# All ten product fields in the first step, in another order, and a quarter of the comparisons on ScalarE in three steps

## What is computed

```python
e = jnp.stack([tbl_0[ids[:, 0]], tbl_1[ids[:, 1]], ...], axis=1)   # (2048, 26, 128)
combined = jnp.concatenate([e, r_dense_x[:, None, :]], axis=1)     # (2048, 27, 128)
z = jnp.einsum('bfd,bgd->bfg', combined, combined)[:, _TRIU_I, _TRIU_J]
h = jnp.concatenate([z, r_dense_x], axis=1)                        # 351 + 128
h = jnp.maximum(h @ W_top1 + b_top1, 0.0)                          # 479 x 512
h = jnp.maximum(h @ W_top2 + b_top2, 0.0)                          # 512 x 256
y = h @ W_top3                                                     # 256 x 1
```

## Time and profile before

| | us |
|---|---|
| time, median of 3 runs (363.35 to 363.50) | 363.44 |
| profiled execution, its own time | 364.55 |
| its span, first to last instruction | 362.7 |
| PE busy | 333.9 (92%) |
| POOL busy | 255.9 (71%) |
| DVE busy | 232.7 (64%) |
| ACT busy | 130.4 (36%) |
| mean granted PE clock, share of full | 0.986 |

### The profile page before, as it was taken

One profiled execution on the slowest core, in us unless ns is written; L12 is line 12 of the kernel. 1 busy time (PEld: TensorE's weight loads), 2 busy tenths in 40 slices (PEclk: granted clock), 3 DMA queues, 4 the chain that ended last, 5 costly groups with the idle time before them and its releaser, 6 DMA issues.

```text
span 362.7 us, 9532 instructions
## 1 busy us (share of the span) xinstructions
PE 333.9 (92%) x4024; PEld 311.0 (86%) x4024; DVE 232.7 (64%) x358; ACT 130.4 (36%) x225; POOL 255.9 (71%) x271
## 2 busy tenths in 40 slices
PE   0578898999999999999999999999999999869896
PEld 0578888788999989999999989999999989858795
DVE  5998696698668928696668928695668925110010
ACT  3486364322233323332243323332343223231422
POOL 5777787777777777777777777777777777777300
PEclk9999899999999999999999999999999999978999
DMA  6998258343343414444353424343343224234220
GB/s 174 249 256 222 69 129 247 92 114 72 93 126 107 119 52 114 110 121 100 93 131 108 115 53 129 97 123 95 102 125 105 72 58 129 61 111 123 50 72 2
DMA packets 31440, 41.01 MB, mean 113 GB/s; under 512 B 16959, under 2 KB 23823, under 8 KB 31398
## 3 DMA queue, kind: packets, MB, share of 16 engines
q1 hardware_dynamic: 21827, 22.44, 22.7%
q0 software_dynamic: 8448, 17.32, 18.3%
q10 hardware_dynamic: 1123, 0.64, 0.7%
HBM read 33.01 MB, written 7.36 MB: 111 GB/s over the span
## 4 chain that ended last, share of the span: by engine, by line
PE 79%; POOL 9%; DMA 5%; issue 3%; ACT 2%; DVE 1%; ACTq 0%; SPq 0%
PE ps_o L645 35%; PE ps_g L672 16%; PE ps_l L696 10%; POOL rows L248 9%; PE ps_t L657 7%; PE ps_l L722 6%; PE ps_l L698 3%; DMA rows<-tbl,idx 3%; PE ps_l L742 1%; ACT emb L392 1%; DMA idx<-ids_g 1%; DMA turn<-gram 1%; PE ps_l L733 1%; DMA z<-turn 1%; PE ps_o L713 0%
## 5 line engine op out<-in xcount | busy, mean ns | idle before, releaser
L248 POOL DMA_INDIRECT rows<-tbl,idx x264 | 255.0, 966 | 82.8 <-issue 78.1
L549 DVE TENSOR_SCALAR onehot<-ids_b,row_of 125x513 fp32r<-125x513 int16 x296 | 196.1, 739 | 14.2 <-PE ps_o L645 9.7
L645 PE MATMUL ps_o<-onehot,tab 125*128 125x256 f32 x1216 | 160.2, 289 | 16.2 <-DVE tab L539 13.0
L645 PEld LDWEIGHTS ps_o<-onehot,tab 125*128 125x128 f32 x1216 | 150.3, 191 | 19.9 <-issue 15.9
L563 DVE COPY gram<-ps_g 128x432 f32<-128x432 f32 x32 | 19.4, 608 | 88.0 <-PE ps_g L672 78.8
L672 PEld LDWEIGHTS ps_g<-emb 128*54 128x54 f32 x2048 | 58.0, 138 | 10.2 <-ACT emb L392 5.6
L672 PE MATMUL ps_g<-emb 128*54 128x54 f32 x2048 | 61.5, 222 | 4.4 <-ACT emb L392 4.4
L385 ACT COPY emb<-ps_o 128x512 f32<-128x512 f32 x38 | 30.3, 796 | 97.4 <-PE ps_o L645 97.4
L392 ACT COPY emb<-ps_t 128x512 f32<-128x512 f32 x66 | 43.2, 676 | 4.6 <-PE ps_t L657 4.3
L657 PE MATMUL ps_t<-ident,rows 128*128 128x128 f32 x264 | 38.9, 276 | 4.8 <-DMA rows<-tbl,idx 3.5
L696 PE MATMUL ps_l<-z,w_sb 117*128 117x256 f32 x168 | 40.9, 379 | 0.2 <-issue 0.2
(11 more groups left out here) (30 smaller groups left out, 65.8 us busy)
## 6 DMA issues: line engine op xcount, KB each, us to landing
turn<-gram SPq DMA_DIRECT2D x62, 91.1 KB
ids_b<-ids_oh SPq DMA_DIRECT2D x35, 129.0 KB, 3.5
stage<-tbl SPq DMA_DIRECT2D x10, 448.0 KB
rows<-tbl,idx POOLq DMA_INDIRECT x264
z<-turn SPq DMA_DIRECT2D x64, 40.5 KB
turn<-gram SPq DMA_DIRECT2D x62, 21.1 KB
xs<-x SPq DMA_DIRECT2D x8, 128.0 KB, 2.1
z<-turn SPq DMA_DIRECT2D x45, 4.5 KB
```

Source lines behind the costliest of these rows:

```text
L248: nc.gpsimd.indirect_dma_start(out=rows[m % RING][:, i, :], out_offset=None, in_=gathered[GATHERED.index(f)] if f in GATHERED else oh_tabl ...
L549: nc.vector.tensor_scalar(onehot[n % BUFS][0:OH_P, 0:FILL].rearrange("p (a b) -> p a b", a=RUNS), ids_b[0:OH_P, o, :, 0:RUN], row_of[0:OH_ ...
L645: last = nc.tensor.matmul(ps_o[n % 2][:, j, :], tab[0:OH_P, UNIT * o + j, part, h, :], onehot[m % BUFS][0:OH_P, STEP * j:STEP * (j + 1)], ...
```

## The change

Step 0 now makes all five units by products, so the first two tiles have four quads like the others and POOL issues 256 gathers. The units of steps 0 and 1 are interleaved, in the order

```diff
-ACT_STEPS = 2
+ACT_STEPS, ACT_FILLS = 3, 2
+DVE_FILLS = FILLS - ACT_FILLS
...
 def act_makes(t, h):
-    return t < ACT_STEPS and h == FILLS - 1
+    return t < ACT_STEPS and h >= DVE_FILLS
...
             def load_ids(t, o):
-                if t and o < units_of(t - 1):
-                    sp.wait_ge(onehot_made, made_by_dve(t - 1, o, FILLS - 1))
-                    if act_makes(t - 1, FILLS - 1):
-                        sp.wait_ge(onehot_act, made_by_act(t - 1, o))
+                s = ids_before(t, o)
+                if s is not None:
+                    sp.wait_ge(onehot_made, made_by_dve(s, o, last_made(s)))
+                    if act_makes(s, FILLS - 1):
+                        sp.wait_ge(onehot_act, made_by_act(s, o, FILLS - 1))
...
-            for n in range(2):
+            for n in range(6):
                 load_chunk(n)
-            sp.dma_start(idx[:, FIRST_NQ:, :], ids_g[:, FIRST_NQ:, :]).then_inc(idx_in[1], 16)
+            load_ids(0, 3)
+            sp.dma_start(idx[:, NQ:, :], ids_g[:, NQ:, :]).then_inc(idx_in[1], 16)
             load_x(0)
-            for n in range(2, NOH):
-                load_chunk(n)
-                if n == NOH - 3:
-                    load_ids(1, 3)
-                    load_ids(1, 4)
-                    for o in range(FIRST_UNITS):
-                        load_ids(1, o)
+            load_chunk(6)
+            load_chunk(7)
+            load_ids(0, 4)
+            load_chunk(8)
+            load_chunk(9)
+            load_ids(1, 1)
+            load_ids(1, 2)
+            for dst, src in ((b1_sb, b1), (b2_sb, b2), (w3_sb, w3)):
+                sp.dma_start(dst[:], src).then_inc(small_in, 16)
+            load_ids(1, 3)
+            load_ids(1, 4)
             load_x(1)
             load_ids(2, 0)
             spread(0)
...
                 fetch_z(2 * t - 1)
+                if t == STEPS - 1:
+                    store_y(t - 2)
...
-                if t + 1 < STEPS:
+                if t + 2 < STEPS:
                     store_y(t - 1)
...
+            def first_unit():
+                for j in range(UNIT):
+                    for part in range(2):
+                        pe.wait_ge((chunk_h, chunk_l)[part], j + 1)
+                        for h in range(FILLS):
+                            if j + part == 0:
+                                if act_makes(0, h):
+                                    pe.wait_ge(onehot_act, made_by_act(0, 0, h))
+                                else:
+                                    pe.wait_ge(onehot_made, made_by_dve(0, 0, h))
+                            last = nc.tensor.matmul(
+                                ps_o[0][:, j, :], tab[0:OH_P, j, part, h, :], onehot[h][0:OH_P, STEP * j:STEP * (j + 1)],
...
```

On ACT, four ids blocks (those of the first four units of the order) are issued at the very start instead of three, and a `make` of two comparisons stands ahead of each `keep_unit` up to step 2, in the loop too:

```diff
                 keep_quad(a, 0)
+                if shared:
+                    make(t + 1, 1)
                 keep_unit(t + 1, 0)
                 keep_quad(a, 1)
+                if shared:
+                    make(t + 1, 2)
                 keep_unit(t + 1, 1)
```

More of the change, by code:

```diff
@@ L133, in tower_kernel @@
         row_made = sem("row_made")
+        row_act_made = sem("row_act_made")
         small_in = sem("small_in")
         idx_in = [sem(f"idx_in{i}") for i in range(2)]
-        ids_in = [sem(f"ids_in{o}") for o in range(UNITS)]
+        ids_in = [sem(f"ids_in{i}") for i in range(UNITS + 1)]
         x_in = [sem(f"x_in{u}") for u in range(2)]
@@ L256, in _ @@
                     pool.wait_ge(idx_in[tile], 16)
-                for k in range(quads_of(tile)):
+                for k in range(NQ):
                     gather(tile, k)
@@ L556, in makes, with makes_of, keep_bank @@
                         make(t, n // FILLS, n % FILLS)
+            def makes_of(n, first, end):
+                t, o = FIRST_ORDER[n]
+                makes(t, FILLS * o + first, FILLS * o + end)
+            def keep_bank(tile, h):
+                if tile and h == 0:
+                    dve.wait_ge(turn_out[(tile - 1) % 2], TURN_DMAS * 16 * ((tile + 1) // 2))
+                dve.wait_ge(gram_done, GBANKS * tile + h + 1)
+                nc.vector.tensor_copy(gram_of(h), products_of(h)).then_inc(gram_kept[h % 2], 1)
             def keep_gram(tile):
-                if tile:
-                    dve.wait_ge(turn_out[(tile - 1) % 2], TURN_DMAS * 16 * ((tile + 1) // 2))
                 for h in range(0, GBANKS, 2):
-                    dve.wait_ge(gram_done, GBANKS * tile + h + 1)
-                    nc.vector.tensor_copy(gram_of(h), products_of(h)).then_inc(gram_kept[h % 2], 1)
+                    keep_bank(tile, h)
             def keep_y(t):
@@ L649, in unit @@
                     last.then_inc(onehot_used, 1)
+            def first_unit():
[10 more added lines that the diff above has]
+                                ps_o[0][:, j, :], tab[0:OH_P, j, part, h, :], onehot[h][0:OH_P, STEP * j:STEP * (j + 1)],
+                                start=(j, part, h) == (0, 0, 0), stop=(j, part, h) == (UNIT - 1, 1, FILLS - 1),
+                                skip_group_check=True)
+                            if (j, part) == (UNIT - 1, 1):
+                                last.then_inc(onehot_used, 1)
             def quad(tile, k):
@@ L757, in _ @@
             pe.wait_ge(gram_zeroed, 2)
-            unit(0, 0)
+            first_unit()
             quad(0, 0)
+            unit(1, 0)
+            quad(0, 1)
             unit(0, 1)
-            quad(0, 1)
+            quad(0, 2)
             unit(0, 2)
-            quad(0, 2)
             quad(0, 3)
-            unit(1, 0)
-            quad(0, 4)
-            products(0)
             unit(1, 1)
             quad(1, 0)
+            unit(0, 3)
+            quad(1, 1)
             unit(1, 2)
-            quad(1, 1)
+            quad(1, 2)
+            unit(0, 4)
+            quad(1, 3)
             unit(1, 3)
-            quad(1, 2)
+            products(0)
             unit(1, 4)
-            quad(1, 3)
-            quad(1, 4)
             products(1)
@@ L842 @@
     arrays["ids_oh"] = np.ascontiguousarray(np.pad(low, ((0, 0), (0, 0), (0, 0), (0, PITCH - RUN))))
-    quads = [(tile, k) for tile in range(TILES) for k in range(quads_of(tile))]
+    quads = [(tile, k) for tile in range(TILES) for k in range(NQ)]
     arrays["ids_g"] = np.ascontiguousarray(np.stack(
```

165 lines of the change are left out of this document (98 added, 67 removed).

## The result

| | before | changed |
|---|---|---|
| time, median of 4 runs each (us) | 363.47 (363.35 to 366.48) | 368.86 (368.19 to 369.77) |
| ratio, with its 95% interval | | 1.013 (1.0073 to 1.0187) |
| profiled execution, its own time | 364.55 | 368.19 |
| its span | 362.7 | 366.4 |
| mean granted PE clock | 0.986 | 0.986 |

The forecast was 361.4 with a range to 366.0; the kernel is 1.3% slower and lies outside.

What follows compares the result with a forecast made beforehand. It took PE and POOL side by side to bound the middle, DVE's comparisons the loop's first step. Terms +4.9 - 3.55 + 1.2 - 2.1 - 2.5 = -2.05 us, from the 363.44 median, gave 361.4; range 355.5 to 366.

Steps and rivals of the forecast that it cites:

- step (5): First layer 1: z of tile 1 lands at 87.6, PE comes at 86.4; +1.2 us, bounds 0 and +4.
- The start, +4.9: Start, laid out on DVE with late ids of (1,1): second products end at 73.2 instead of 68.24, +4.9 us.
- The bound of +0.5: Start: lower bound of the +4.9 us, if the ids are there when DVE comes.
- The early first unit is worth nothing: Start: PE's earlier first unit, near 9 us, gains nothing, since DVE is not moved by it.
- Step (4): Loop's step 1: ScalarE takes a quarter of the comparisons, bringing DVE under PE's 4.3 us a unit; -3.55 us, other bound -1.
- Steps (1) and (6): Tail: eight fewer gathers on POOL end the wait for rows, -2.1 us; products behind run at full clock, -2.5.
- Steps (2) and (7): Ahead of the loop, two units replace two quads, +6.6 us of PE work; moved small loads, table load and store: nothing.
- A: Start: loads faster than 203 KB/us, so ids are in time and most of the z delay goes; 355.8 us, chance 0.22.
- B: Start: ScalarE waits for PE's comparison buffers, 0.75 us in each of six units, +4.5, so 365.9; chance 0.2.
- C: Start, near 31 to 35 us: PE's clock falls to 1.2 GHz for two units, 2.4 us, so 363.8; chance 0.1.
- D: Loop's step 1: the sharing does nothing, -1 instead of -3.55, so 363.9; chance 0.08.

Runs made afterwards that it cites:

- swap: Changed kernel with weights ahead of the first spread, ids of (1, 1) in free buffer 4 ahead of the last two tables, (0, 4) reusing buffer 1: 360.26 us.
- ids early: Changed kernel with the ids of unit (1, 1) loaded ahead of the last two tables instead of behind them: 363.22 us, ratio 0.9953.
- one of eight: Changed kernel with weights ahead of the first spread, (1, 1) ids ahead of the last two tables, and ScalarE making one of eight comparisons: 360.27 us.

## Why the prediction was wrong

**Where it failed: step (5), z of tile 1.** I had seen the mechanism, weights between the fetch of tile 0 and the spread of tile 1, and priced it at +1.2 with +4 as the bound. It was +6.1, and taking the weights away from there gave back 6.0 in step 1. Three pieces were too small. I let the spread be issued at 73.5 and only its data wait; it was issued at 77.70, since SP was still busy with the fetch, the weights and the ids (71.66 to 77.60). I let the data through at 80.4 and landed 2.2 later; they landed at 86.95. And I did not count the clock: I used the rule of the clock at the tail, where PE stands 2 us, and not at the one place where I myself had a wait in front of PE. z came at 91.57 instead of 87.6, and PE 0.9 later than I had it. That a wait of 4 us then costs 1.9 more is also in the start, where the unit behind a stand of 3.23 us took 5.95.

**The start, +4.9, was +5.85.** The chain of my layout is right in its times: DVE through (0, 2) at 29.2 (29.8), ids at 35.37 (34.2), last half ended at 53.75 (52.9), then 20.34 us (20.3). The error is the 1.2 of the load, and there the time was nearer than the reason: I counted the bytes ahead of the block and left out that SP may issue it only when the comparisons of (0, 1) are made, at 23.04. POOL, which I left out of the start too, is its next limit: with the eight gathers back it ends at 80.58. The bound of +0.5 with ids in time was right in kind: with the stand down to 1.4 us the start ended at 69.61, +1.4.

**"The early first unit is worth nothing"** was wrong by a little, 1.0 us: DVE is moved by it, through the comparison buffers that PE frees and through ScalarE's table halves.

**Step (4), -3.55, had the right size and the wrong reason.** Leaving the sharing out of the loop costs 0.4 us of step 1 and nothing in the time. What took away most of it is the lead of five comparisons with which DVE enters the loop, by its new order. I read the 32 in a row as a lack of speed; DVE had stood 5.20 us just before with none of them made. That the size came out to the hundredth is luck.

**Steps (1) and (6), the tail,** -2.1 and -2.5, together -4.6: measured -4.66. Rows in time, products at 3.60, the clock at full. That the number came out says little of the reason: PE came so late to the tail that the rows would have been there with the eight gathers too, as the run that put them back shows. **Steps (2) and (7)** have no term of their own in the sum, and the traces show nothing against them.

**The rivals.** A (ids in time) did not come: 35.37. B (the feeders wait for each other) is there in two places, 1.07 and 1.43 us in front of kept units, not 0.75 in each of six, and one comparison more for DVE is worse than these waits. C (the clock) came as the short dip, one unit of 5.95. D did not come: units of 3.79. The side of the result, slower, came from none of them but from a term of the forecast whose upper bound was 2.1 too low. With that term at its measured 6.1 the sum would have been +2.85 and the sign right. The 0.2% that I took for what a measurement can tell was too fine as well: the interval of this result is 0.57% to each side. The profile mark that I had named for it, "a gap of several us in front of the first layer 1", is what the trace shows.

The cause is settled for the changed kernel: some 6 us at z of tile 1 and 4.1 of the start in one late ids block, each shown by moving it alone. What stays open is how much of the spread's delay is queue order and how much plain sharing of the engines, what DVE's new order is worth alone, and how much a buffer more for the ids would give; none of these was tried.

## What to carry to other kernels

When a change takes slack out of a stage, look in each DMA queue for large loads whose old cover is gone: price both the time the issuing engine spends on them and what their data do to the small transfer behind, and add the clock that a stand of some microseconds costs afterwards. Here 1470 KB ahead of a spread of 449 KB cost 6.1 us, and one 129 KB block behind two tables 4.1; moving both gave 3% without touching a compute instruction. When an engine seems too slow at a boundary, look at what it did just before: it may have stood, with work at hand that its order kept behind a wait.

## What the runs showed of the hardware that was not expected

- A stand of 3.23 us and one of 4.24 us on PE each brought the granted clock to 0.50 and cost 1.9 us behind them (a unit of 5.95 for 4.02; the first 14 matmuls of layer 1 4.94 for 3.03), and one of 4.91 cost 2.9 (9.86 for 6.92). The length of the stand alone does not decide: 2.11 us in the swap was followed by a unit of 5.55, and 0.46 a quad after 1.17 too, while 2.13 in "ids early" and 2.63 in "one of eight" left units of 4.02 and 4.00.
- A spread of 449 KB behind 1470 KB in the same queue landed 6.1 us after its last issue, and 2.7 without them. An ids block of 129 KB issued at 23.0 to 23.2 us landed after 12.31 us behind two tables of 500 KB, and after 7.55 ahead of them.
- One chip ran before at 508.61 us, 11 minutes after it had run it at 364.5, with a mean granted clock of 0.87; the four kernels profiled there show PE starting single matmuls 0.7 to 2.8 us apart for tens of microseconds. The order of kernels seen there doesn't carry over: ScalarE with one of eight had the lowest ratio of the four on it (0.9721) and the highest but for the gathers on the other chip (0.988), though most of these intervals overlap.
